# A graph layer and an LSTM on one Trainium2 core: where the last block's reciprocal root is taken, where three weight splits stand, and how the final test is written

## The reference

```
x = x + gnn(layernorm(x))                    # h = x @ W + b; mean of h[src] over the edges of each dst
x = x + lstm(layernorm(x), one sequence)     # 3125 steps, hidden size 256

def step(h, c):                              # xi, xg, xo = x @ U_* + b_*
    i = sigmoid(xi + h @ V_i)
    g = tanh(xg + h @ V_c)
    o = sigmoid(xo + h @ V_o)
    c = h * c + i * g
    h = o * tanh(c)
```

## Time and profile before

| | us |
|---|---|
| median of 3 runs | 456.59 |
| lowest and highest | 456.39, 458.94 |
| the profiled execution, whole | 457.81 |
| its span, first to last instruction | 455.9 |
| PE busy | 416.8 (91% of the span) |
| DVE busy | 341.6 (75%) |
| ACT busy | 321.5 (71%) |
| POOL busy | 145.9 (32%) |

### The profile page before, as it was taken

How to read it: one execution, slowest core, us unless ns; L and a number is a source line. 1 busy time by engine, 2 the same in 40 slices (tenths; PEclk the granted TensorE clock), 3 DMA queues, 4 the chain that set the end, 5 groups by cost and what they waited for, 6 DMA issues and landing times.

```text
span 455.9 us, 15425 instructions
## 1 busy us (share of the span) xinstructions
PE 416.8 (91%) x6114; PEld 368.5 (81%) x6114; DVE 341.6 (75%) x1095; ACT 321.5 (71%) x906; POOL 145.9 (32%) x249
## 2 busy tenths in 40 slices
PE   4987899999999999999999999998888889999992
PEld 3666787878898999899998989887777778888882
DVE  4989887996997868777786833627577778888885
ACT  1668696577776767667676853564788888888881
POOL 6740420153432435233422412312123222322320
PEclk9989799999999999999999999999999999999997
DMA  8375001331100001000100010000000000210112
GB/s 186 70 156 140 0 1 51 104 104 31 58 2 1 1 4 55 1 2 1 58 2 1 2 39 20 0 3 22 38 4 4 4 3 4 61 51 12 61 60 62
DMA packets 9603, 16.90 MB, mean 37 GB/s; under 512 B 2006, under 2 KB 7451, under 8 KB 9526
## 3 DMA queue, kind: packets, MB, share of 16 engines
q1 hardware_dynamic: 8230, 14.60, 11.0%
q0 software_dynamic: 880, 0.86, 0.9%
q10 hardware_dynamic: 416, 0.39, 0.5%
HBM read 6.23 MB, written 9.61 MB: 35 GB/s over the span
## 4 chain that ended last, share of the span: by engine, by line
PE 64%; DVE 18%; ACT 7%; issue 7%; DMA 2%; POOL 0%; SPq 0%; DVEq 0%; ACTq 0%; POOLq 0%
PE bank L1244 13%; PE bank L1246 13%; PE bank L1328 10%; PE bank L1436 9%; PE bank L1238 6%; PE bank L1356 4%; ACT tc L1099 3%; PE bank L1278 3%; DVE h L1913 3%; DVE hots L1691 3%; DVE h L1950 3%; DVE c_st L1908 2%; DMA x_sb<-in_x_dram 2%; PE bank L1472 1%; PE bank L1304 1%
## 5 line engine op out<-in xcount | busy, mean ns | idle before, releaser
L1238 PE MATMUL bank<-hots 128*128 128x125 f16 x625 | 119.7, 222 | 0.3 <-DVE hots L1691 0.2
L1691 DVE TENSOR_TENSOR hots<-iota,kp 128x1000 f16<-128x1000 f16 x160 | 106.5, 693 | 12.0 <-PE bank L1238 11.9
L1436 PE MATMUL bank<-h,V 128*128 128x62 f16 (+1 forms) x2952 | 101.1, 192 | 13.0 <-DVE h L1913 8.4
L1436 PEld LDWEIGHTS bank<-h,V 128*128 128x128 f16 x2952 | 93.0, 97 | 24.2 <-issue 22.8
L1244 PE MATMUL bank<-h_flat,counts 125*128 125x257 f16 x375 | 96.7, 273 | 0.2 <-ACT counts L934 0.2
L1246 PE MATMUL bank<-h_flat,counts 125*128 125x256 f16 x375 | 95.8, 271 | 0.0
L934 ACT ACTIVATE counts<-bank 125x500 f16<-125x500 f32 x96 | 55.2, 602 | 20.8 <-PE bank L1238 19.7
L1244 PE MATMUL bank<-h_flat,gx 125*128 125x257 f16 x250 | 68.2, 274 | 0.0
L1246 PE MATMUL bank<-h_flat,gx 125*128 125x256 f16 x250 | 67.5, 270 | 0.0
L824 POOL TENSOR_TENSOR hc<-h_flat,c_st 128x126 f32<-128x126 f32 x80 | 34.0, 425 | 95.7 <-DVE c_st L1908 84.9
L1238 PEld LDWEIGHTS bank<-hots 128*128 128x128 f16 x625 | 57.1, 98 | 7.8 <-DVE hots L1691 0.6
(11 more groups left out here) (185 smaller groups left out, 781.2 us busy)
## 6 DMA issues: line engine op xcount, KB each, us to landing
h_dram<-h_flat SPq DMA_DIRECT2D x1, 3137.2 KB
x_dram<-x_sb SPq DMA_DIRECT2D x5, 625.0 KB
x_sb<-in_x_dram SPq DMA_DIRECT2D x5, 560.0 KB
out_dram<-x_sb SPq DMA_DIRECT2D x4, 560.0 KB
out_dram<-x_sb SPq DMA_DIRECT2D x1, 336.0 KB
x_sb<-in_x_dram SPq DMA_DIRECT2D x5, 65.0 KB
out_dram<-x_sb SPq DMA_DIRECT2D x4, 65.0 KB
gx<-in_L_gnn_weight_dram ACTq DMA_DIRECT2D x1, 256.0 KB, 3.8
```

The lines of the kernel that those rows point to most:

```text
L1238: nc.tensor.matmul(ps_count[group % 3][:, pos * KEYS:(pos + 1) * KEYS], hots[:, ring, 0, g // 2, :, g % 2], hots[:, ring, 1, g // 2, 0:KEY ...
L1436: mm = nc.tensor.matmul(to[:, m % (2 * HH) * n:(m % (2 * HH) + 1) * n], V16[:, v_part, d, m * P:(m + 1) * P], h16[:, h_part, d, c0:c1], st ...
L1691: nc.vector.tensor_tensor(hots[:, k % RING, :, :, 0:KEYS, :].rearrange("p a h n g -> p (a h) n g"), iota[:, 0:KEYS, :].unsqueeze(1).to_bro ...
```

## The change

There are four edits.

1. The root of turn 24 is taken on POOL by `root`, as for the other turns, and `last_root` is gone. On POOL it stands ahead of the `hc` of early turn 24.
2. PE's transposition of the last block's `z` moves from place 635 to place 632, which is ahead of the 24 products of early turn 24.
3. The low parts of U move from places 64, 71 and 77 to 69, 74 and 79.
4. The final test has no squares. For each of the cells of half 0, the cells of half 1 and all states it makes two passes, "new - tol <= old" and "new + tol >= old", each one instruction with an accumulator that counts the hits into a column of `near` of its own. One of the six stands in the last turn ahead of the state of half 0, two ahead of the state of half 1. PE sums the six columns with six accumulating matmuls, each of which waits for its column, and the flag is compared with twice the count.

```diff
-        near = sb("near", [P, 1])
+        near = sb("near", [P, NEAR_TESTS])
...
-        LAST_AT = {FINISH_AT: (561, 580, 605, 630), NORM_AT: (575, 587, 622, 632), TURN_AT: (576, 588, 625, 635),
+        LAST_AT = {FINISH_AT: (561, 580, 605, 630), NORM_AT: (575, 587, 622, 632), TURN_AT: (576, 588, 625, 632),
...
-            for turn in range(BLOCKS - 1):
+            for turn in range(BLOCKS):
...
-                if turn >= 3:
+                if 3 <= turn < BLOCKS - 1:
                     early_old_part(turn - 2)
...
-                            pe.wait_ge(near_ready, 1)
-                            nc.tensor.matmul(ps_one[0:1, 0:1], near[:, :], ones[:, 0:1], start=True, stop=True
-                                             ).then_inc(near_ps, 1)
+                            for a in range(NEAR_TESTS):
+                                pe.wait_ge(near_ready, a + 1)
+                                mm = nc.tensor.matmul(ps_one[0:1, 0:1], near[:, a:a + 1], ones[:, 0:1],
+                                                      start=(a == 0), stop=(a == NEAR_TESTS - 1))
+                            mm.then_inc(near_ps, 1)
...
             def second_norm(j, turn):
-                if turn == BLOCKS - 1:
-                    last_root(j)
...
-            UV_LOW = {64: 0, 71: 1, 77: 2, 128: 3, 152: 4, 165: 5}
+            UV_LOW = {69: 0, 74: 1, 79: 2, 128: 3, 152: 4, 165: 5}
...
+            def test_near(new, old, k0, k1, bound):
...
+                nc.vector.scalar_tensor_tensor(out=near_hits[:, a, :, 0:k1 - k0], in0=new[:, :, k0:k1], scalar=bound,
+                                               in1=old[:, :, k0 + 1:k1 + 1], op0=ALU.add,
+                                               op1=ALU.is_le if bound < 0 else ALU.is_ge, accum_out=near[:, a:a + 1]
+                                               ).then_inc(near_ready, 1)
...
                     if (t, q) == (DONE, 1):
-                        cell_gap()
+                        test_cells(1, -STATE_TOL)
+                        test_cells(1, STATE_TOL)
...
+                    if (t, q) == (DONE, 0):
+                        test_cells(0, -STATE_TOL)
                     state_next(q, t)
...
+            test_cells(0, STATE_TOL)
+            test_states(-STATE_TOL)
+            test_states(STATE_TOL)
```

More of the change, by code:

```diff
@@ L225, in bass_gnn_lstm_kernel @@
         gate_w, ig_w, hc_w, tc_w = whole(gate, MT), whole(ig, HH), whole(hc, HH), whole(tc, HH)
[L228 to L230 removed]
+        NEAR_TESTS = 6
+        near_hits = counts_all[:, :, :, :].rearrange("p r t n -> p (r t n)")[:, 0:2 * NEAR_TESTS * HH * (CHUNKS - 1)].bitcast(
+            F32).rearrange("p (a m k) -> p a m k", a=NEAR_TESTS, m=HH)
+        near = sb("near", [P, NEAR_TESTS])
         far_i = sb("far_i", [1, 1], I32)
@@ L1957, in counted_edge, with test_cells, test_states @@
                 edges_set[0] += 1
-            def cell_gap():
+            near_tests = [0]
+            def test_near(new, old, k0, k1, bound):
+                a = near_tests[0]
+                near_tests[0] += 1
+                nc.vector.scalar_tensor_tensor(out=near_hits[:, a, :, 0:k1 - k0], in0=new[:, :, k0:k1], scalar=bound,
+                                               in1=old[:, :, k0 + 1:k1 + 1], op0=ALU.add,
+                                               op1=ALU.is_le if bound < 0 else ALU.is_ge, accum_out=near[:, a:a + 1]
+                                               ).then_inc(near_ready, 1)
+            def test_cells(half, bound):
+                dve.wait_ge(c_ready[half], POST)
+                test_near(c_st[:, c_after(DONE), :, :], c_st[:, C_START, :, :], COLS[half][0],
+                          min(COLS[half][1], CHUNKS - 1), bound)
+            def test_states(bound):
                 for half in range(2):
-                    dve.wait_ge(c_ready[half], POST)
-                counted_op(nc.vector.tensor_tensor(gap[:, 1, :, :], c_st[:, c_after(DONE), :, 0:CHUNKS - 1],
-                                                   c_st[:, C_START, :, 1:CHUNKS], ALU.subtract))
+                    dve.wait_ge(h_ready[half], POST)
+                test_near(h_after(DONE), h_start, 0, CHUNKS - 1, bound)
             outs = [0]
@@ L1996, in _ @@
                     if (t, q) == (DONE, 1):
-                        cell_gap()
+                        test_cells(1, -STATE_TOL)
+                        test_cells(1, STATE_TOL)
                     else:
-                        for step, d in out_parts(t, q)[:LAST_OUTS[q]]:
+                        for step, d in out_parts(t, q)[:1]:
                             add_out(step, d)
+                    if (t, q) == (DONE, 0):
+                        test_cells(0, -STATE_TOL)
                     state_next(q, t)
@@ L2005, in _ @@
                     link(nc.vector.tensor_copy(open_i[:, :], open_f[:, :]))
[L2006 to L2011, removed]
-            link(nc.vector.tensor_tensor(gap[:, 0, :, :], gap[:, 0, :, :], gap[:, 0, :, :], ALU.mult))
-            gap_all = gap[:, :, :, :].rearrange("p a m k -> p (a m k)")
-            nc.vector.scalar_tensor_tensor(out=gap_all, in0=gap_all, scalar=STATE_TOL ** 2,
-                                           in1=ones[:, 0:1].to_broadcast([P, 2 * HH * (CHUNKS - 1)]), op0=ALU.is_le,
-                                           op1=ALU.mult, accum_out=near[:, :]).then_inc(near_ready, 1)
+            test_cells(0, STATE_TOL)
+            test_states(-STATE_TOL)
+            test_states(STATE_TOL)
             for d in range(HH):
```

4 lines of the change are left out of this document (1 added, 3 removed).

## The result

| | kernel before | changed kernel |
|---|---|---|
| median of the runs timed side by side | 457.91 us (20 runs, 456.39 to 459.55) | 458.91 us (20 runs, 457.62 to 459.82) |
| the profiled execution, its span | 457.81, 455.9 us | 459.05, 457.2 us |
| mean granted clock of TensorE | 0.983 | 0.985 |

The ratio is 1.002, with a 95% interval of 1.0011 to 1.0029: the changed kernel is slower, by 0.9 us (0.5 to 1.3). The forecast was -0.04 us. More runs stand behind the median of before now than the three that the prediction knew, so the forecast is held against the difference and not against 456.5.

A forecast was written before the change was run, and what follows sets the result against it. DVE was taken to bound the stretch at 90 to 100 us and the final test, PE then ACT turn 24. The terms +0.5 + 0 - 0.54 = -0.04 on the 456.59 median gave about 456.5 us, range 455.3 to 457.9.

The forecast's parts named there:

- Part 2: Last block's transposition ahead of turn 24's products: PE stalls for `z`, +0.5 us, bounds +0.3 and +1.0.
- Part 1: Turn 24's root on POOL: takes 1.62 us, so the last block's `z` ends 0.29 us earlier, at 319.27.
- It costs nothing: Turn 24's `hc`, queued behind the POOL root, is done at about 319.6, before its reader needs it: no cost.
- part 4: The new final test at the program's end: last sum ready at 449.53 instead of 450.07, -0.54 us, between -0.9 and -0.25.
- The quiet power: In turn 24's POOL root: the power takes 551 ns, as where DVE left POOL alone, because DVE is idle.
- slow-power rival: Turn 24's root on POOL is no faster than DVE's: 0.5 us more, 457.0 us; chance 0.10.
- Part 3: U's low parts later, near 92 us: PE's wait moves from first `z` to second; 0, bounds -0.66 and +0.1.
- rival of a kept head start: Between 94 and 100 us: PE keeps the 0.66 us from the earlier first `z`; 455.9 us; chance 0.10.
- The push by the first pass: Final test, last turn: the pass beside POOL's `hc` delays half 0's state and all behind it by 0.18 us.
- The reads: Final test: reading the accumulator costs each pass 0 to 0.08 us more.
- half-rate rival: Final test: passes reading two full tensors with an accumulator cost twice, +1.04 us, 457.6 us; chance 0.08.
- The stall is hidden: Turn 24: slack absorbs PE's stall for `z`, leaving only the end's gain, 456.05 us; chance 0.06.

The follow-up runs named there:

- after_hc_first: The changed kernel with `hc` of turn 24 issued ahead of the last root on POOL instead of behind it; ratios 1.0016 and 0.9998 (458.13 and 457.5 us).
- after_busy: The changed kernel with 16 matmuls into an unread bank on PE ahead of the last block's transposition; 457.62 us, ratio 1.0005.
- hc_first_busy: The changed kernel with `hc` of turn 24 ahead of the last root on POOL and 16 unread matmuls ahead of the transposition; 457.04 us, ratio 0.9998.

## Why the prediction was wrong, point by point

**Part 2 is the step that failed.** It put the stall at "+0.5" and let every matmul behind it run at the rate of the earlier trace rows. The runs showed +2.27 us. What failed in it is above all the rate of the matmuls behind the stall, which the working left at full clock. What goes beyond +0.5, 1.77 us, has three shares:

- **The clock, +1.40.** The working never asked whether PE's clock survives the stall, and none of the rivals had it. The profile before gave a warning that I read only as a wait: PE stood still for 1.40 us ahead of the same products already, and the change lengthens that wait by half. The same trace also shows the clock fall elsewhere, and what that costs (rows below): the same six matmuls took 0.72 us from start to start of the next at a clock of 1.00 and 1.34 at 0.50. The chain has 24 + 12 + 3 + 12 matmuls behind the stall, 3.2 us, so up to nearly as much again. A rival on the slower side, somewhere from +1 to +3 us, belonged there.
- **The `z`, +0.20.** Part 1 had it end 0.29 us earlier than the root on DVE. It started 0.09 us earlier than forecast but took 0.29 longer beside `hc`. "It costs nothing" looked only at who waits for `hc`, not at what runs beside it; part 4 priced such a neighbour, part 1 didn't. after_hc_first shows the 0.29 alone.
- **The start of U's products, +0.17.** I took their old start from the chain (321.58), which counts a piece only from the end of the one ahead; PE's timeline has them at 321.42. With 0.64 for 0.48, less the 0.10 by which the `z` of after_hc_first comes earlier than forecast, 0.54 would be due there, and +0.57 was measured. The rest of the working held: from the transposition to U's products 2.74 us were forecast (319.32 to 322.06), and 2.74 are in the profile of after_hc_first (318.60 to 321.34).

The clock's fall near 48 us in the trace of the kernel before, PE's timeline and three windows:

```profile
46.13 0.88 PE L1278 MATMUL bank<-gx 128*125 128x256 f16 x6
46.85 0.27 PE L1284 MATMUL bank<-h_flat,minus_one 125*125 125x256 f16 x1
48.20 0.68 PE L1258 MATMUL bank<-ident,gx 125*128 125x125 f32 x2 [1.08 <-POOL gx L757]
...
49.63 1.54 PE L1278 MATMUL bank<-gx 128*125 128x256 f16 x6
50.97 0.42 PE L1284 MATMUL bank<-h_flat,minus_one 125*125 125x256 f16 x1
```

```profile
46.00:47.00 1.00, 1.00 (x8) 0.76 (x8) 0.90 (x5) 0.79 (x3) 0.27 (x1) 1.00 0.00 0
...
48.00:49.00 1.00, 0.80 (x6) 0.74 (x6) 1.00 (x3) 0.38 (x2) 1.00 (x2) 0.50 0.00 0
49.00:50.00 1.00, 1.00 (x6) 0.58 (x5) 0.98 (x3) 0.89 (x2) 1.00 (x2) 0.50 0.00 0
```

The wait here is 1.08 us, shorter than the 1.40 that left the clock at 1.00 in turn 24; but two more, of 0.84 and 0.43 us, end shortly ahead of it, at 44.81 and 45.91, while in turn 24 PE is 0.8 or more busy in each microsecond up to the wait. So the length of one wait alone does not tell whether the clock falls.

**Part 1**, the root itself: right, and 0.07 us shorter than taken. The quiet power (0.55 us) was the one to take, and the slow-power rival is out.

**Part 3: 0.** Right, with the mechanism as told. The rival of a kept head start is out: DVE is the bound there.

**Part 4: -0.54** had the mechanism right and the size off, -0.94 being just beyond its lower bound of -0.9. The push by the first pass, put at 0.18, was 0.01: the pass took 0.52 us as feared and ended 0.14 behind its `hc` (448.78 against 448.64; the row had given 0.15, the prediction's other price was 0.29), but the state moved by only 0.09 (0.85 us behind its cell, 0.76 before), and the cell of half 1 by 0.01 (1.39 behind the cell of half 0, 1.38 before). The reads cost nothing, where I had taken the middle of 0 to 0.4, some 0.17. The starts were 0.04 closer. The half-rate rival is out: 0.29 us against its limit of 0.35. The rule of the Trainium skill's "Vector Engine (DVE) Microarchitecture Reference", section "Points that are easy to get wrong", that it rested on doesn't show in these passes: both inputs are f32 tensors in SBUF, and 0.28 and 0.29 us at 122 to 126 columns is what a state without an accumulator takes.

**The stall is hidden**: out. after_busy shows 0.87 us of it on the path at full clock.

**The range.** Taken as a difference, +0.9 lies within the 1.3 us that the range allowed on the slower side, but by luck: that end was made of the passes at half rate, which did not come, while part 2 stood in it with +0.5 and not with its own bound of +1.0. The clock was in no term of it.

## What to carry to other kernels

When an edit makes TensorE wait longer, price the work behind the wait at both clock levels, and look at the granted clock in windows of a microsecond, not at the mean, first of all in the trace that you already have: it may show a fall and its price elsewhere. If a late operand can go behind work that is ready, leave it there. And when work is queued behind a producer on GpSimd, ask what VectorE will do at that moment, since its next instruction may run beside it.

## What the runs showed of the hardware

- In turn 24 TensorE's clock fell to 0.50 some 0.3 to 1.2 us after work resumed behind a wait of 2.04 to 2.13 us (five profiles of five), in one of four behind 1.76 us, and in none of seven behind 1.40 us. In all of them PE had been 0.8 or more busy in each microsecond up to the one in which the wait begins. It stood at 0.50 for about three microseconds of unbroken work and came back. The Trainium skill's "TensorE: Matmul & The Clock Gate", section "HAM oscillation — how this bites in real kernels", warns of idle times longer than any of these; these profiles differ from it.
- Near 48 us the clock fell in all 18 profiles, in before behind waits of 0.84, 0.43 and 1.08 us close together; so the waits of turn 24 are no limits for other places.
- Sixteen matmuls into an unread bank during the wait kept the clock at 1.00: in after_busy, whose kernel without them had the fall in four profiles of four, and in hc_first_busy, without them one of four.
- A `z` of 125x256 in f32, with one tensor and two columns of scalars as inputs, took 0.70 us beside POOL's `hc` and 0.41 alone. The Trainium skill's "SBUF — State Buffer", section "Who interferes with whom", says that a VectorE instruction with at most one SBUF input, outside certain modes, does not contend with GpSimd; if the columns of scalars don't count as inputs, the 0.70 us differs from that, and no run here tells whether they count. An earlier `z` of the kernel before, at 296.23 us, took 0.41 although an `hc` began beside it 0.16 us later, and there POOL's took 0.81; in these two cases, and for the first pass of the final test (0.52 us, begun 0.03 behind its `hc`), the one that started second was the slower.
- An instruction on VectorE with two f32 tensors and an accumulator costs no more than one without: 0.29 us at 122 columns, 0.41 at 248.
